# Post-norm attention and dense mixture-of-experts layer on eight cores: the two expert weight tiles are single-buffered, and the first activation tiles and the Q and K weights of each half are loaded ahead

## The reference

```python
x = layernorm(x + attn(x))        # 16 heads of 64, window of 7 keys, projections 1024 x 1024
x = layernorm(x + ffn(x))

def ffn(x):                       # 8 experts, 1024 -> 4096 -> 1024, all of them dense
    logits = x @ gate_w + gate_b
    top_w, top_i = top_k(logits, 2);  top_w = softmax(top_w)
    comb = zeros.at[rows, top_i].add(top_w)
    out = 0
    for ei in range(8):
        h = relu(x @ w1[ei] + b1[ei])
        out = out + comb[:, ei:ei + 1] * (h @ w2[ei] + b2[ei])
    return out
```

## Time and profile before

| what | us |
|---|---|
| timed runs, two of them | 5095.41 and 5768.04, median 5431.73 |
| profiled execution, own time | 5127.53 |
| its span, first to last instruction on the slowest core (core 2) | 5126.0 |
| spans of the eight cores | 5081.1 to 5126.0 |
| mean granted TensorE clock of the cores | 0.887 to 0.895 |

### The profile page before, as it was taken

The page is one execution under the profiler, slowest core; times in us unless marked ns, Lnnn a source line. Parts: engine busy times, 40 slices in busy tenths (PEclk is TensorE's granted clock), DMA queues, the critical chain, the costliest instruction groups (busy, mean ns, idle before and its releaser), DMA issues. The chain is left out here.

```text
span 5126.0 us, 53179 instructions; the slowest of 8 cores (5081.1 to 5126.0 us)
## 1 busy us (share of the span) xinstructions
PE 4322.3 (84%) x19260; PEld 1923.7 (38%) x19624; DVE 1087.8 (21%) x2736; ACT 1174.4 (23%) x2462; POOL 146.6 (3%) x176
## 2 busy tenths in 40 slices
PE   5744489999999999999575444999999999999996
PEld 2221234444444444444232222344444444444442
DVE  0233311221122112112202333121122112211112
ACT  2323222112211211121333233212211221111122
POOL 0000000000000000000000000000000000000000
PEclk9755579999999999999876555899999999988998
DMA  5100064545454444444140000634343434333430
GB/s 84 17 9 13 5 96 69 83 66 83 69 80 70 79 73 76 74 74 66 48 76 5 9 13 7 106 70 79 69 83 66 82 66 82 68 65 66 78 70 33
DMA packets 149770, 310.94 MB, mean 61 GB/s; under 512 B 3641, under 2 KB 4025, under 8 KB 149453
## 3 DMA queue, kind: packets, MB, share of 16 engines
q0 software_dynamic: 144096, 289.49, 34.0%
q1 hardware_dynamic: 5422, 18.03, 1.1%
HBM read 588.60 MB, written 8.39 MB: 116 GB/s over the span
## 5 line engine op out<-in xcount | busy, mean ns | idle before, releaser
L853 PE MATMUL m_pY<-m_w2b,m_hg 128*128 128x512 bf16 x8028 | 1789.6, 382 | 81.8 <-ACT m_hg L830 73.0
L813 PE MATMUL m_pH<-s_xt,m_w1b 128*128 128x512 bf16 x8028 | 1790.0, 382 | 9.5 <-issue 0.7
L830 ACT ACTIVATE m_hg<-m_pH,s_b1pc 128x512 bf16<-128x512 f32 x1024 | 703.5, 687 | 2900.0 <-PE m_pH L813 2900.0
L868 DVE SCALAR_TENSOR_TENSOR m_acc<-m_pY,s_comb,m_acc 128x512 f32<-128x512 f32 x1024 | 721.7, 747 | 3022.3 <-PE m_pY L853 2927.2
L853 PEld LDWEIGHTS m_pY<-m_w2b,m_hg 128*128 128x128 bf16 x8192 | 801.7, 98 | 1069.7 <-issue 169.1
L813 PEld LDWEIGHTS m_pH<-s_xt,m_w1b 128*128 128x128 bf16 x8192 | 806.4, 98 | 985.4 <-issue 66.6
L442 PE MATMUL h_pj<-h_v_tm,h_attnT 128*128 128x64 bf16 x256 | 54.3, 212 | 284.0 <-DVE s_rSt L412 186.8
L380 DVE SCALAR_TENSOR_TENSOR h_smx<-h_pj,s_consts,s_masks 128x134 f32<-128x134 f32 x256 | 90.1, 352 | 480.0 <-PE h_pj L370 479.8
L261 PE MATMUL h_pj<-h_xt_ext,h_wbuf 128*128 128x512 bf16 (+1 forms) x626 | 116.4, 341 | 51.1 <-PEq L57 50.4
L442 PEld LDWEIGHTS h_pj<-h_v_tm,h_attnT 128*128 128x128 bf16 x256 | 26.5, 104 | 324.4 <-issue 324.4
L615 PE MATMUL h_ptb<-s_id_bf,h_o_sb 128*128 128x128 bf16 x128 | 26.9, 271 | 125.8 <-POOL h_o_sb L603 108.8
(11 more groups left out here) (84 smaller groups left out, 1184.2 us busy)
## 6 DMA issues: line engine op xcount, KB each, us to landing
m_w1b<-w POOLq DMA_DIRECT2D x64, 2048.0 KB, 16.4
m_w2b<-w POOLq DMA_DIRECT2D x64, 2048.0 KB, 16.2
h_x_own<-xh SPq DMA_DIRECT2D x16, 512.0 KB, 3.7
out<-s_ostg SPq DMA_DIRECT2D x16, 512.0 KB, 2.6
h_xb<-xh POOLq DMA_DIRECT2D x16, 256.0 KB, 4.0
h_wbuf<-wq POOLq DMA_DIRECT2D x2, 2048.0 KB, 17.8
h_wbuf<-wk POOLq DMA_DIRECT2D x2, 2048.0 KB, 28.2
h_wbuf<-wv POOLq DMA_DIRECT2D x2, 2048.0 KB, 15.5
```

The lines of the kernel that those rows point to most:

```text
L813: e.matmul(pH[jj % 2][:, 0:512], w1b[par][:, ic * GCOLS + j * 128: ic * GCOLS + j * 128 + 128], xt1[:, ic * HALF_T + ts * 512: ic * HALF_T ...
L830: e.activation(hg[:, j * HALF_T + ts * 512: j * HALF_T + ts * 512 + 512], pH[jj % 2][:, 0:512], AF.Relu, bias=b1pc[:, e_i * 32 + g_i * 8 + ...
L853: e.matmul(pY[t % 2][fs][:, 0:512], hg[:, j * HALF_T + t * 128: j * HALF_T + t * 128 + 128], w2b[par][:, j * GCOLS + fs * 512: j * GCOLS + ...
L868: e.scalar_tensor_tensor(acc[:, t * D + fs * 512: t * D + fs * 512 + 512], pY[t % 2][fs][:, 0:512], comb[:, t * 8 + e_i: t * 8 + e_i + 1], ...
```

## The change

`xb` and `wbuf` move to the outer scope, which lives through the whole kernel. To make room, `w1b` and `w2b` get one buffer each in place of two. A new function `emit_prefetch(h)` issues four DMAs on POOL's queue: the first two blocks of the activations of half h, `wq` and `wk`. It is called once behind the setup, so that its four DMAs are the first of block A1 of half 0, and once behind the 32 steps of M of half 0, for half 1. The loads of step s of M now wait for mm1 or mm2 of step s-1. The semaphores by parity stay, as does everything in A2, A3 and L2.

```diff
+        xb = sb("xb", [128, 2 * D], BF16)
+        wbuf = [sb("wbuf0", [128, 8 * D], BF16), sb("wbuf1", [128, 8 * D], BF16)]
...
+        def emit_prefetch(h):
+            B_ = h * HALF_T
+            for t in range(2):
+                rows = 128
+                src_ = xh_d.ap()[B_ + t * 128: B_ + t * 128 + rows, :]
+                pre[(h, "xld", t)] = p.op(
+                    "pool",
+                    lambda e, t=t, src_=src_:
+                    e.dma_start(xb[0:128, (t % 2) * D:(t % 2) * D + D], src_),
+                    inc="sXB%d" % (t % 2), k=16)
+            pre[(h, "wq")] = p.op("pool", lambda e: e.dma_start(
+                wbuf[0][:].rearrange("p (c n) -> p c n", c=8),
+                wq_d.ap().rearrange("(c p) n -> p c n", p=128)), inc="sWQ0", k=16)
+            pre[(h, "wk")] = p.op("pool", lambda e: e.dma_start(
+                wbuf[1][:].rearrange("p (c n) -> p c n", c=8),
+                wk_d.ap().rearrange("(c p) n -> p c n", p=128)), inc="sWQ1", k=16)
+
+        emit_prefetch(0)
...
-                emit_xld(0)
-                emit_xld(1)
+                xld[0] = pre[(half, "xld", 0)]
+                xld[1] = pre[(half, "xld", 1)]
...
-                wq_ev = p.op("pool", lambda e: e.dma_start(
...
+                wq_ev = pre[(half, "wq")]
+                wk_ev = pre[(half, "wk")]
                 p.flush("A1_h%d" % half)
...
-                w1b = [sb2("w1b0", [128, NJ * GCOLS], BF16), sb2("w1b1", [128, NJ * GCOLS], BF16)]
-                w2b = [sb2("w2b0", [128, NJ * GCOLS], BF16), sb2("w2b1", [128, NJ * GCOLS], BF16)]
+                w1b = [sb2("w1b0", [128, NJ * GCOLS], BF16)]
+                w2b = [sb2("w2b0", [128, NJ * GCOLS], BF16)]
...
-                        if step >= 2:
-                            wl.append(h_ev[(step - 2, 15)])
+                        if step >= 1:
+                            wl.append(h_ev[(step - 1, 15)])
...
-                        if step >= 2:
-                            wl.append(y_ev[(step - 2, 7, 1)])
+                        if step >= 1:
+                            wl.append(y_ev[(step - 1, 7, 1)])
...
+                if half == 0:
+                    emit_prefetch(1)
                 moe_last["mm1"] = h_ev[(31, 15)]
```

More of the change, by code:

```diff
@@ L166, in build_nc @@
                     "hrelu14": None, "hrelu15": None}
+        pre = {}
+        def emit_prefetch(h):
[15 more added lines that the diff above has]
+        emit_prefetch(0)
         for half in range(2):
@@ L173, in build_nc @@
                 ps1 = lambda n, s, d: S1.enter_context(nc.psum_tensor("h%d_" % half + n, s, d))
-                xb = sb1("xb", [128, 2 * D], BF16)
                 xt_ext = sb1("xt_ext", [128, 8 * EXT], BF16)
@@ L178, in build_nc @@
                 v_tm = sb1("v_tm", [128, 9 * D], BF16)
-                wbuf = [sb1("wbuf0", [128, 8 * D], BF16),
-                        sb1("wbuf1", [128, 8 * D], BF16)]
                 x_own = sb1("x_own", [128, 2 * D], F32)
@@ L776, in build_nc @@
                             "pool",
-                            lambda e, e_i=e_i, g_i=g_i, par=par:
+                            lambda e, e_i=e_i, g_i=g_i:
                             e.dma_start(
-                                w1b[par][:].rearrange("p (c n) -> p c n", c=8),
+                                w1b[0][:].rearrange("p (c n) -> p c n", c=8),
                                 w1_d.ap()[e_i, :, g_i * GCOLS:(g_i + 1) * GCOLS]
                                 .rearrange("(c p) n -> p c n", p=128)),
-                            waits=wl, inc="sW1%d" % par, k=16)
+                            waits=wl, inc="sW1%d" % (step % 2), k=16)
                         wl = []
-                        if step >= 2:
-                            wl.append(y_ev[(step - 2, 7, 1)])
+                        if step >= 1:
+                            wl.append(y_ev[(step - 1, 7, 1)])
                         elif moe_last["mm2"] is not None:
@@ L789, in build_nc @@
                             "pool",
-                            lambda e, e_i=e_i, g_i=g_i, par=par:
+                            lambda e, e_i=e_i, g_i=g_i:
                             e.dma_start(
-                                w2b[par][:].rearrange("p (c n) -> p c n", c=8),
+                                w2b[0][:].rearrange("p (c n) -> p c n", c=8),
                                 w2_d.ap()[e_i, g_i * GCOLS:(g_i + 1) * GCOLS, :]
                                 .rearrange("(c p) n -> p c n", p=128)),
-                            waits=wl, inc="sW2%d" % par, k=16)
+                            waits=wl, inc="sW2%d" % (step % 2), k=16)
                         for j in range(NJ):
@@ L813, in build_nc @@
                                         e.matmul(pH[jj % 2][:, 0:512],
-                                                 w1b[par][:, ic * GCOLS + j * 128:
-                                                          ic * GCOLS + j * 128 + 128],
+                                                 w1b[0][:, ic * GCOLS + j * 128:
+                                                        ic * GCOLS + j * 128 + 128],
                                                  xt1[:, ic * HALF_T + ts * 512:
@@ L855, in build_nc @@
                                                     j * HALF_T + t * 128 + 128],
-                                                 w2b[par][:, j * GCOLS + fs * 512:
-                                                          j * GCOLS + fs * 512 + 512],
+                                                 w2b[0][:, j * GCOLS + fs * 512:
+                                                        j * GCOLS + fs * 512 + 512],
                                                  start=(j == 0), stop=(j == NJ - 1)),
```

## The result

The changed kernel takes 5058.02 us in the median of 11 runs, the kernel before 5095.78 us in the median of the 10 runs beside it. The ratio is 0.9923 with a 95% interval of 0.9911 to 0.9936. That is 39 us off (33 to 45), where 41.8 us were forecast. The profiled execution takes 5055.61 us. Against the 5127.53 us of the profiled execution before it seems to gain 72 us, but there core 2's PE had a granted clock of 0.95 from 4300 to 4600 us and of 0.87 from 4600 to 4800 us, in M of half 1, where it is 1.00 after; the ratio does not rest on that execution.

A forecast was written before the change was run, and what follows sets the result against it. PE's own work was taken to bound M, with block ends outside it waiting for POOL's open loads. Gains of 32.2 + 9.6 + 0 = 41.8 us off 5127.53 us gave 5085.7 us, range 5038 to 5120 us.

The forecast's parts named there:

- the lower timed run: Whole kernel before the change: the lower of two timed runs, 5095.41 us; the same gain gives 5054 us from it.
- Half 1: Start of half 1: prefetch ahead of the block's end removes waits of 8.6 and 23.6 us, 32.2 us in all.
- Half 0: Block A1 of half 0: weights ahead of the third activation block let A2 start at 68.6 us, gaining 9.6 us.
- bounds of 2.9 and 25.5 us: Half 0's gain: 2.9 us if both weights need 30.0 us, 25.5 us if the third block isn't held up.
- The bound that counted 30.0 us for the pair: Block A1, half 0: wq and wk need 30.0 us from 19.3 us, A2 starts at 75.3 us, gain 2.9 us.
- Rival 1: Half 0: third activation block isn't held up by the weights, gain there 25.5 us, total 5069.8 us; chance 0.17.
- Block M: M's steps: single-buffer loads land within 18.1 us, with 28.9 or 27.6 us available; cost 0 us.
- the 19 us that were given as a sign: Block M: landings staying under 19 us would show the forecast right.
- Rival 3: Block M: loads are exposed and landings beyond 28 us stall PE 124 times; 5687 us if landings doubled; chance 0.04.
- The end of M: Half 0: prefetch lands by 2493.5 us, or 2500 us; L2 starts at 2509.19 us and isn't held up.
- Rival 2: Block's end: the wait isn't the load, or prefetch delays M's end; 5127.5 or 5118.9 us; chance 0.11.

The follow-up runs named there:

- the run whose release came behind the sixth block: Changed kernel with the load of w1b held back until six of mm2's eight token blocks are done; 5632.6 us in the fastest of three runs.
- the late releases: Changed kernel, w1b's load held until the second, fourth or sixth of mm2's eight token blocks: 5054.85, 5154.69 (faster of its two repeats) and 5632.6 us (fastest).

## Why the prediction was right

The direction, the size of the gain and the range held: a gain of 41.8 us was forecast, and 39 us (33 to 45) were measured. The time itself came out 28 us below the forecast, 5058.02 us in place of 5085.7 us, because the forecast stands on the profiled execution of 5127.53 us, which the prediction took for one of a kind with the lower timed run; it was longer by the clock in M of half 1. From the lower timed run the prediction has 5054 us by the same sum, and that is where the measured times lie. Point by point:

- **Half 1, 32.2 us forecast.** The timeline shows 31.3 us, the run with this part alone 32 us (25 to 39). The conclusion that a block's end waits for POOL's open loads, which the profile didn't name, is shown by the run with wk in A2.
- **Half 0, 9.6 us forecast.** The timeline shows 4.9 us; this term was too large by half, inside its own bounds of 2.9 and 25.5 us. What failed is the step that lets the pair take 2 x 11.6 = 23.2 us from the landing of the first blocks. It took 47.8 - 20.9 = 26.9 us: wk landed 12.6 us behind wq, and wq 35.2 - 20.9 = 14.3 us behind the first blocks. The third block started at 49.24 us, not at 44.0 us; PE waited 21.26 us for it, where some 17 us were forecast. Another 1.6 us of this is not of the change: the first blocks came at 20.90 us here and at 19.28 us before, and over the cores they come between 16.0 and 20.9 us in both kernels. The bound that counted 30.0 us for the pair was the better value.
- **Order in the queue.** Rival 1 needed the third block to pass the weights. It landed 1.2 us behind wk. The Trainium skill, "DMA: Bandwidth & Descriptors", section "Two DMAs through the same engine are not ordered", has descriptors of one queue and engine start in order; this trace agrees, and the freedom that the section leaves across engines didn't show at this size.
- **Block M, 0 us forecast.** Ratio 0.9997 with the single buffers alone, and no wait for a load. The slowest landing was 19.2 us, a little over the 19 us that were given as a sign. Rival 3 exists as a mechanism: no wait below the limit, and above it more than the excess at which it was priced, since mm1 also runs at the lower clock behind each wait. The advice to double-buffer (the Trainium skill, "Trainium Kernel Development and Optimization", section "Best Practices") fits the run whose release came behind the sixth block, with 453.6 us of waits, and not the changed kernel, where a load has some 10 us in hand.
- **The end of M.** Forecast: the prefetch lands by 2493.5 us and L2 isn't held up. It landed at 2491.8 us, and L2 started 0.33 us behind M as before. That the two times lie so close is luck: this core was some 6 us ahead (L2 at 2503.11 us, not at 2509.19 us), and w2(31) and the four loads needed 2491.8 - 2445.86 = 45.9 us from the issue of w2(31), where 42.7 us were forecast from its release. The block's end had 11 us in hand.
- **Rival 2** (the wait isn't the load, or the prefetch holds M up) fell with the run with wk in A2 and with the start of L2.

## What to carry to other kernels

A wait that the profile puts down to the end of a block can be a load which the next block doesn't need yet: compare the moment it ends with the landing of every load still open, not only with the one whose data is read. Moving that load behind the block's end got some two thirds of the gain here with one line. Before giving up a second buffer, set the landing of a load against the time in which its buffer rests; where the rest is a whole phase of other work, the second buffer can be spent elsewhere. Take the landing when neighbour cores load in step, which is its slowest here. And a large load put ahead of small ones that the next work needs delays these: two loads of 2 MB made the wait for the third block 21.3 us, where it was 1.7 us.

## What had not been expected

The same 2 MB loads land in very different times. In M of half 0 of the changed kernel the median for w1b was 13.2 us on core 7 and 18.3 us on core 5, in half 1 it was 17.5 and 13.2 us, and in the run with the release behind the sixth block 12.8 to 13.1 us on all eight cores. So it does not belong to the core. The traces point at the neighbour: here are the issues of one load of w1b on core 4 and on core 5, in half 0, then in half 1.

```profile
1002.79 0.87 POOL L793 DMA_DIRECT2D m_w1b<-w  x1 [26.75 <-PE m_pH L828]
1002.69 0.87 POOL L793 DMA_DIRECT2D m_w1b<-w  x1 [26.75 <-PE m_pH L828]
...
3504.60 0.87 POOL L793 DMA_DIRECT2D m_w1b<-w  x1 [26.75 <-PE m_pH L828]
3514.68 0.87 POOL L793 DMA_DIRECT2D m_w1b<-w  x1 [26.75 <-PE m_pH L828]
```

0.1 us apart, the two cores' medians are 17.9 and 18.3 us; 10.1 us apart, they are 13.0 and 13.2 us. Cores 6 and 7 do the reverse: 6.8 us apart in half 0 (14.3 and 13.2 us), 0.1 us apart in half 1 (17.9 and 17.5 us). In the run with the release behind the sixth block cores 4 and 5 issue one of their first loads 1.1 us apart, and it lands in 16.6 and 18.5 us; the waits, longer on the core whose load is slower, drive them 25 us apart, and the landings fall to 12.9 and 13.1 us. That would explain why the late releases cost less than landings of 17 us. It is read from the traces, with each core's time counted from its own first instruction; no run set the distance of two cores. A cover worked out from one run's landings holds for that run.

The stretch in which the Q projection of half 0 begins reads a granted clock of 1.00, while its matmuls come at a lower rate (stretches of core 5, two of the kernel before, then after: start:end, length, busy us of PE and PEld with counts, clock, DMA share, GB/s):

```profile
78.00:80.00 2.00, 1.54 (x4) 0.58 (x5) 1.00 0.00 0
80.00:82.00 2.00, 2.00 (x7) 0.77 (x6) 1.00 0.00 0
...
73.00:75.00 2.00, 1.76 (x5) 0.69 (x6) 1.00 0.00 0
75.00:77.00 2.00, 2.00 (x6) 0.66 (x5) 1.00 0.00 0
77.00:79.00 2.00, 2.00 (x6) 0.76 (x5) 1.00 0.00 0
79.00:81.00 2.00, 2.00 (x10) 0.87 (x9) 1.00 0.00 0
81.00:83.00 2.00, 2.00 (x11) 0.87 (x9) 1.00 0.00 0
```

Six matmuls in 2 us are about half of the 11 that follow, for nearly 6 us, where the same core showed it for about 4 us before. In half 1 the same start reads 0.50. So early in the span the count of matmuls says more than the clock column, and by these counts some 1 us of half 0's gain was given back there (an estimate).
